# Attention with kept keys in the third phase: GpSimd pauses during VectorE's threshold moves, ScalarE's signs in two spans of 13, PSUM reads ahead of the moves

## What is computed

```python
attn = jax.nn.softmax(scores, axis=-1)                # 16 heads of width 8, 256 x 256
sr = MIN_SPARSITY + (1.0 - MIN_SPARSITY) * jax.nn.sigmoid(entropy_ema - entropy_threshold)
k_keep = jnp.maximum(1, (L * (1.0 - sr)).astype(jnp.int32))      # one number a head
order = jnp.argsort(-attn, axis=-1)
rank = jnp.argsort(order, axis=-1)
keep = rank < k_keep[None, :, None, None]
w = jnp.where(keep, attn, jnp.float32(0.0))
w = w / (jnp.sum(w, axis=-1, keepdims=True) + 1e-10)
out = jnp.einsum('bhqk,bhkd->bhqd', w, v)
return out.transpose(0, 2, 1, 3).reshape(B, L, D) @ Wo.T + bo
```

## Time and profile before

| | |
|---|---|
| median of 3 runs | 2914.39 us (2909.72 to 2918.05) |
| the profiled execution: its time, its span | 2914.69 us, 2912.8 us |
| busy in the span: TensorE, VectorE, ScalarE, GpSimd | 2258.8, 1924.8, 1082.0, 666.0 us |
| the chain that ended last, by engine | PE 50%, DVE 31%, issue 7%, ACT 6%, POOL 3% |
| DMA over the span | 49.02 MB, mean 17 GB/s |

### The profile page before, as it was taken

How to read it: one execution, slowest core, us unless ns; L and a number is a source line. 1 busy time by engine, 2 the same in 40 slices (tenths; PEclk the granted TensorE clock), 3 DMA queues, 4 the chain that set the end, 5 groups by cost and what they waited for, 6 DMA issues and landing times.

```text
span 2912.8 us, 42629 instructions
## 1 busy us (share of the span) xinstructions
PE 2258.8 (78%) x13648; PEld 1725.5 (59%) x13648; DVE 1924.8 (66%) x5803; ACT 1082.0 (37%) x3168; POOL 666.0 (23%) x900
## 2 busy tenths in 40 slices
PE   4999999962566676656699999499579999999604
PEld 2777777741455565555566666277347777778501
DVE  5567453245788787887466666455558777777587
ACT  1333333338666777663122222033223333333100
POOL 3333121032664557555100000331000000000000
PEclk7999999965555555555599999599689999999658
DMA  3111000020000000000100000110100000000000
GB/s 107 36 30 39 18 21 24 1 81 21 6 11 7 12 12 6 6 1 1 41 1 0 0 0 0 40 41 25 56 10 1 0 0 0 0 0 0 1 0 15
DMA packets 57561, 49.02 MB, mean 17 GB/s; under 512 B 6840, under 2 KB 55704, under 8 KB 56856
## 3 DMA queue, kind: packets, MB, share of 16 engines
q1 hardware_dynamic: 54340, 45.50, 4.9%
q10 hardware_dynamic: 3040, 1.38, 0.3%
HBM read 19.78 MB, written 1.05 MB: 7 GB/s over the span
## 4 chain that ended last, share of the span: by engine, by line
PE 50%; DVE 31%; issue 7%; ACT 6%; POOL 3%; SPq 1%; ACTq 1%; DVEq 0%; DMA 0%; POOLq 0%
PE bank L1139 8%; PE bank L1555 4%; PE bank L1547 4%; PE bank L1548 4%; DVE weights L2543 4%; PE bank L1021 3%; PE bank L1001 3%; PE bank L1293 2%; DVE small L2581 2%; PE bank L1277 2%; ACT rope_s L3346 2%; ACT rope_c L3346 2%; PE bank L1120 2%; PE bank L1014 2%; PE bank L1096 2%
## 5 line engine op out<-in xcount | busy, mean ns | idle before, releaser
L1461 PE MATMUL bank<-V,probsT 128*128 128x9 f32 x1024 | 234.5, 362 | 86.8 <-ACT probsT L3357 86.8
L1461 PEld LDWEIGHTS bank<-V,probsT 128*128 128x128 f32 x1024 | 224.6, 326 | 124.8 <-ACT probsT L3357 105.6
L2184 DVE TENSOR_REDUCE nmax<-bank 128x4 f32<-128x1024 f32 x144 | 176.2, 1223 | 113.1 <-PE bank L1096 112.1
L3174 ACT ACTIVATE probs<-bank,nmax 128x256 f32<-128x256 f32 x256 | 118.7, 469 | 222.6 <-DVE nmax L1936 222.6
L1555 PEld LDWEIGHTS bank<-weights,hid 128*128 128x128 f32 x1152 | 151.0, 192 | 79.0 <-issue 75.5
L3410 ACT ACTIVATE hid<-bank 128x512 f32<-128x512 f32 x144 | 85.6, 597 | 283.2 <-PE bank L1548 271.8
L2777 DVE TENSOR_TENSOR hid<-hid,bank 128x512 f32<-128x512 f32 x144 | 98.7, 688 | 127.2 <-PE bank L1555 123.0
L1555 PE MATMUL bank<-weights,hid 128*128 128x128 f32 x1152 | 152.4, 276 | 12.9 <-DVE hid L2777 10.5
L1001 PE MATMUL bank<-big,qT 128*128 128x256 f32 x512 | 142.1, 404 | 15.4 <-DVE x L1857 14.8
L1547 PE MATMUL bank<-O,weights 128*128 128x512 f32 x288 | 150.1, 603 | 2.6 <-DVE big L2717 2.6
L1548 PE MATMUL bank<-O,weights 128*128 128x512 f32 x288 | 148.0, 596 | 0.0
(11 more groups left out here) (615 smaller groups left out, 5666.5 us busy)
## 6 DMA issues: line engine op xcount, KB each, us to landing
qT<-parts SPq DMA_DIRECT2D x276, 32.0 KB
big<-V SPq DMA_DIRECT2D x192, 32.0 KB
big<-parts SPq DMA_DIRECT2D x180, 32.0 KB
weights<-in_weights_l_ffn SPq DMA_DIRECT2D x1, 4832.0 KB, 14.1
weights<-in_weights_l_attn SPq DMA_DIRECT2D x1, 3904.0 KB, 12.5
weights<-in_weights_l_ffn SPq DMA_DIRECT2D x1, 3628.0 KB, 15.2
qT<-V SPq DMA_DIRECT2D x96, 32.0 KB
weights<-in_weights_l_ffn SPq DMA_DIRECT2D x1, 2304.0 KB, 7.8
```

Source lines behind the costliest of these rows:

```text
L1461: last = mm(pb[1][:, t * S + h * wide:t * S + (h + 1) * wide], probsT[:, h % 2, at:at + P], values_of(b, k)[:, h * wide:(h + 1) * wide], s ...
L2184: V_.tensor_reduce(to, scored.rearrange("p (i a n) -> p i a n", i=HPG, n=n), AX.X, ALU.max, negate=True).then_inc(score_max.sem, 1)
L3174: last = nc.scalar.activation(probs[:, h % 3, at:at + n], bank[:, at:at + n], ACT.Exp, bias=nmax[:, h, t:t + 1], accum_out=rowsum[:, h, t: ...
```

## The change

Five edits, all in the four lists of this phase:

1. GpSimd waits for `mid_ready` of move 1 before the candidates of groups 4 and 5.
2. GpSimd waits for `mid_ready` of move 2 before `guess`.
3. On VectorE `l1_intake` and `l1_result` come before move 1 and its count, where they came after.
4. On VectorE `l1_spread` comes before `settle_on`, where it came after.
5. On ScalarE the 26 signs of the second count are two spans of 13 (after heads 0, 1 and after heads 2, 3) in place of 9, 9 and 8 (after heads 0, 1, after 2, 3 and after 4, 5). In the first count the last 12 signs are split in 4 and 8, with `l1_take_normed` and `l1_take_out` between them.

```diff
@@ GpSimd, l1_attn
                         for g in range(2):
                             drop(n, g)
+                        if now(n + 1):
+                            pool.wait_ge(mid_ready.sem, mid_ready(ph, n + 1, 1))
                         for g in range(CANDS, CANDS + 2):
                             candidates(n, g)
...
                     if now(n + 2):
+                        pool.wait_ge(mid_ready.sem, mid_ready(ph, n + 1, 2))
                         guess(n + 2)
@@ VectorE, l1_attn
                     l1_pair(n, 0, (0, 1), (2,))
-                    if now(n + 1):
-                        try_between(n + 1, 1)
-                        count_above(n + 1, 1)
                     if now(n + 3):
                         l1_intake(n + 3)
                     if now(n - 1):
                         l1_result(n - 1)
+                    if now(n + 1):
+                        try_between(n + 1, 1)
+                        count_above(n + 1, 1)
                     l1_pair(n, 2, (), (3,))
...
                     l1_pair(n, 6, (8,), (9, 10, 11))
+                    if now(n + 3):
+                        l1_spread(n + 3)
                     if now(n + 1):
                         settle_on(n + 1)
-                    if now(n + 3):
-                        l1_spread(n + 3)
@@ ScalarE, l1_attn
                     if now(n + 1):
-                        l1_count(n + 1, 0, 20, ROWS1)
+                        l1_count(n + 1, 0, 20, 24)
                     if now(n + 3):
                         l1_take_normed(n + 3)
                     if now(n - 1):
                         l1_take_out(n - 1)
+                    if now(n + 1):
+                        l1_count(n + 1, 0, 24, ROWS1)
...
-                        if now(n + 1) and h < 6:
-                            first = ROWS_DVE + h // 2 * 9
-                            l1_count(n + 1, 1, first, min(first + 9, ROWS1))
+                        if now(n + 1) and h < 4:
+                            first = ROWS_DVE + h // 2 * 13
+                            l1_count(n + 1, 1, first, first + 13)
```

## The result

The changed kernel takes 2890.36 us (median of 4 runs, 2887.06 to 2892.41) against 2914.7 us before in the same comparison (4 runs, 2909.72 to 2918.05). The ratio is 0.9917, with a 95% interval of 0.990 to 0.9934. The forecast was 2888.5 us within 2879 to 2901.

A forecast was written before the change was run, and what follows sets the result against it. VectorE was taken as the bound, its steps with two SBUF inputs waiting for GpSimd's running instruction. Gains of 20 + 3.4 + 3 - 0.5 = 26 us took the 2914.4 us median to 2888.5 us, range 2879 to 2901.

The forecast's parts named there:

- the first move: VectorE, round 3: with GpSimd paused, three waits for drop instructions; ends at 1023.5 instead of 1026.9, 3.4 us earlier.
- The second move: VectorE, round 3: starts 6.4 us earlier but meets GpSimd's drops in four waits; ends at 1050.1 instead of 1053.5.
- The bound beside it: Upper bound per round: if no step of the second move waits, ScalarE's path gives 3.6 us instead of 3.4.
- The signs: ScalarE's second count in spans of 13: counts in 10 us earlier, so head 7's scores become the next limit.
- The PSUM reads: VectorE's intake and result before the first move: not held up beside the drops, putting VectorE another 1.1 us ahead.
- the early round: Round before round 0: 1.0 us lost through head 7's maximum and a ScalarE copy, 0.5 gained by the spread.
- `l1_spread`: VectorE, before the last move: its 0.53 us fit inside the 6.32 us idle time, saving 0.5 us a round.
- The sum: Whole phase: 20 us in rounds 0 to 4, 3.4 in round 5, 3 in round 6, less 0.5: 26 us.
- the slow steps aren't GpSimd's doing: Rival: the first move keeps its 8.8 us and the kernel gets slower, 2919 or 2930 us; chance 0.03.
- GpSimd's chain: Rival: restart, `add_out` and the split take 1.5 us more a round, giving 2899 us; chance 0.12.
- The rule that the pair is held for the whole instruction: Rival from the Trainium skill: the 5.5 us power blocks VectorE's two-SBUF-input steps; 20 us more gain, 2869 us; chance 0.01.
- nothing is won: Rival: head 7's late scores and the drops, both 3 us worse, eat the second move's gain; 2911 us; chance 0.04.

The follow-up runs named there:

- `guess` first: The changed kernel with `guess` and then the second pause put ahead of GpSimd's drops of groups 4 and 5: 2880.39 us (one run).
- half-size run: The kernel before the change, with GpSimd's candidates and drops written as twice as many instructions of half the size (128x256): 2907.15 us.

## Why the prediction was right

*What bounds the kernel, and the first move.* Right. The steps wait for GpSimd's running instruction: halving the instruction halves the wait, and the pause ends it. I had the end of the first move at 17.7 us into the round; it is 17.95. Three waits were forecast and three came, but the first fell on L2496, which has one input in SBUF and which I had taken as free. It ends 0.03 us after a drop instruction. That L2495 ended 0.01 us from the end of an instruction was too exact: taken one by one, the instruction ended at 1019.43 and the step at 1019.48. GpSimd was to stand 1.5 us and stood 1.79.

*The second move.* Right in its mechanism and 0.4 us short. Start forecast 38.7 us into the round, measured 38.63, behind the scores of head 7 as said. Drops to end at 43.0, they end at 43.2. After them I counted 1.28 us of steps and it took 1.5: four waits came as forecast, but the first held L2496, so L2510 was still to be done. Length forecast 5.6, measured 6.09. The bound beside it was wrong: if no step of this move waited, a round was to gain 3.6 us in place of 3.4. With `guess` first none waits, and the last move begins 4.5 us earlier than before (60.9 us into the round, 65.3 before) against 3.0 with the change. ScalarE's path, which I had put 2.3 us earlier, came out 2.9 us earlier (its third count begins 45.1 us into the round in place of 48.0), and its wait for head 9 could go as well.

*The signs.* The chain of links was right, but its worth was not said plainly. My sum already held that the drops take 3 of the 6.4 us; the run with 9, 9 and 8 shows that at most 0.2 us a round of this edit is left.

*The PSUM reads.* That they aren't held up was right. But moving them ahead gains nothing in rounds 1 to 4: the 1.1 us that VectorE is ahead are lost again at the drops, for which the second move waits either way. What the prediction missed is the early round. I took 1.0 us lost there, for head 7 and ScalarE's copy. The measured loss of the whole round is 2.7 us net of `l1_spread`, against 0.5 forecast. The intake ahead of the move lets GpSimd's split start under the move, and its subtractions (L783, L785) run beside it:

```profile
672.33 1.05 DVE L2496 TENSOR_SCALAR small<-small 128x26 f32<-128x26 f32 x1 [0.97 <-ACTq L3353]
...
674.30 1.18 DVE L2504 COPY_PREDICATED small<-small 128x64 f32<-128x64 int32 x1
...
677.12 0.19 DVE L2519 TENSOR_TENSOR small<-small 128x32 f32<-128x32 f32 x1
```

```profile
671.49 0.61 POOL L782 CAST parts<-kT 128x512 bf16<-128x512 f32 x1 [10.69 <-DVE kT L2433]
672.19 1.15 POOL L783 TENSOR_TENSOR kT<-kT,parts 128x512 f32<-128x512 f32 x1
...
674.16 1.24 POOL L785 TENSOR_TENSOR kT<-kT,parts 128x512 f32<-128x512 f32 x1
```

These are of the changed kernel's early round; again L2496, with one input, is held. The move lasts 4.98 us where it lasted 2.34; with the reads behind it lasts 2.33 again. I had written that GpSimd cuts nothing in that round, which is true, and had not asked what else it would now start.

*`l1_spread`.* Right, 0.5 us a round. Its new wait of 2.85 us for TensorE was not foreseen, and cost nothing.

*The sum.* Forecast 26 us; the phase gives 19.9, the profiled executions 22.3, the medians 24.3. By rounds: 4.15 in round 0 (forecast 4.0), 3.2 to 3.5 in rounds 1 to 4 (4.0), 2.4 in round 5 (3.4), 2.5 in round 6 (3.0), and -2.7 in the early round (-0.5). Nearly every term was too large, and the phase fell 6 us short of the forecast. That the median of 2890.36 us lies only 1.9 us from 2888.5 is luck: over 4 us of its gain are not the phase's, and no run shows where they come from.

*The rivals.* That the slow steps aren't GpSimd's doing is refuted by the half-size run. GpSimd's chain, which a rival had 1.5 us later, was 0.2 us late. The rule that the pair is held for the whole instruction is refuted for the power by two runs. That nothing is won is refuted by the result.

## What to carry to other kernels

Where a dependent chain of small VectorE operations slows to the length of GpSimd's instructions, one wait on GpSimd at the right place may give more than any new order of work: here one wait alone gave 17.1 of 22.6 us. Better still is to give GpSimd work in that time that doesn't hold VectorE: with the power there, the seven rounds fell by another 10.3 us. And whoever moves an operation ahead must ask what its result releases, and beside what that will run; the same reordering that changed nothing in rounds 1 to 4 cost 2.7 us where it released GpSimd under a chain that had run alone.

## What was not expected of the hardware

VectorE and GpSimd don't take turns to equal cost. A step of 0.2 us took up to 1.3 us, while four of GpSimd's drop instructions took 5.12 and 5.06 us beside the two moves and 5.07 us away from them. In the early round the second subtraction of the split took 1.24 us beside the move, where it takes 1.16 in round 3; the first took 1.15.
Besides additions, predicated copies (1.23 us) and operations with a scalar and two tensors (1.08 us) are held. So is L2496, which has one input in SBUF and a length of 0.18 us: 1.05 us in the early round, 0.82 in the second move of round 3, each time to 0.03 or 0.04 us after the end of GpSimd's instruction. So two inputs in SBUF are not the only condition. Yet a reciprocal, with one input too, kept its 0.35 us in all moves of all twelve profiles, and operations that read one input from PSUM theirs (0.41 us). What sets these apart no run here tests.
A power of 5.5 us on 128x32 holds nothing, though it has two inputs in SBUF as the drops have. The Trainium skill (SBUF — State Buffer, Terms, the shared port pair) would have it held for the full instruction. For the drops and candidates the traces agree with it; for the power they don't, and the measurement decides. Whether it is the power or its small tile that makes the difference, no run here tells: the drops are 128x512 or 128x256, and no other long instruction was tried on 128x32.
